# A folded last transform, a new end of attention, edge values by DMA, and two short products moved

## The chip, the cores and the metric

The kernel runs on one core of one Trainium2 chip. The metric is the device time of one execution in microseconds (us); all times here are in us unless marked otherwise.

## The reference, cut to what matters

Input `x` is (4, 16, 16, 192) in fp32: four images of 256 places and 192 channels. Four layers follow each other.

- Layer 0 and layer 2 are transformer blocks on windows of 14 x 14: norm, q, k, v, attention of 12 heads of 16 channels with relative positions in rows and columns, softmax, projection, residual; then norm, an MLP of 768 hidden channels with GELU, residual. 16 is not a multiple of 14, so each image gives one whole window and narrow windows on the right and at the bottom (the edges, filled up with padding).
- Layer 1 is a spectral layer with a 2-D real FFT over the places, a block-diagonal two-layer complex MLP, a soft threshold and the inverse FFT.
- Layer 3 is a spectral layer with a Hartley transform over all four axes (images, rows, columns and channels):

```python
def _dht(x):
    f = jnp.fft.fftn(x)
    return f.real + f.imag
X_k  = _dht(x);  X_nk = jnp.roll(jnp.flip(x, (1, 2)), (1, 1), (1, 2))
a, an = X_k[:, r0:r1, :kept], X_nk[:, r0:r1, :kept]          # 16 x 9 modes
o1_k  = relu(0.5*(a@w1[0] - an@w1[1] + a@w1[1] + an@w1[0]) + b1[0])   # o1_nk likewise
o2_k  = 0.5*(o1_k@w2[0] - o1_nk@w2[1] + o1_k@w2[1] + o1_nk@w2[0]) + b2[0]
o2_nk = 0.5*(o1_nk@w2[0] - o2_k@w2[1] + o1_nk@w2[1] + o2_k@w2[0]) + b2[1]
s = o2_k + o2_nk;  s = sign(s) * max(abs(s) - 0.01, 0)
out = _dht(full_with_s) / full.size + x
```

## The kernel before

Each engine has a written-out program of its own, and semaphores order them. The order of the work within an engine is the order in the code. All tensors stay on chip; the DMA queue of SyncE (SP) loads weights and stores the result.

**Attention (`attention(l)`, run for l = 0 and 1).** The tokens are 8 tiles of 128. The norm is done in two halves g of 4 tiles: VectorE takes means and variances (L1332, L1350, L1352), ScalarE the root (L1191), VectorE normalises (L1359), TensorE transposes (`turn_norm`, L751), and ScalarE and VectorE write the result with scale and bias to `yT` (L1196, L1338). `project` (L776) makes q and k: 3 chunks of 128 columns by 2 parts of 512 tokens. 192 channels are 128 and 64, so each of the 6 jobs has one whole product of 128 rows and one short product of 64 rows, both in L791; first all whole ones, then all short ones. `project_values` (L810, L816) makes v. Two jobs `v_edge` (L797) make v again for the edge places, out of a copy of `yT` in window order that POOL makes (L650). `relate` (L834) makes the relative terms, whose last take-out is VectorE's L1398. The list `PROJ` names these jobs; job j uses bank (4 + j) % 8 and waits until job j - 8 has been taken out.

Then 18 groups follow (`GROUPS`: slot of four heads by image or edge window). The edge groups are the 9th to the 14th. For each group TensorE makes scores (`score`, L875, banks 0 to 3), VectorE takes their maxima (L1408, L1411) and turns them (L1426), SP copies the turned maxima into rows of the operand by four DMAs (L628), TensorE makes the scores again transposed and with the maximum subtracted (`turn`, L903, banks 4 to 7), ScalarE takes exponentials (L1250), TensorE weighs the values (`weigh`, L916, bank 4, the last group bank 7), ScalarE takes that out (`take_weighed`, L1241), VectorE inverts the sums (`invert`, L1434 to L1440) and POOL divides (`divide`, L688 to L697). `out_project` (L762) follows per image. The last groups run without scores beside them. After the last `weigh` come `take_weighed`, ScalarE's table load for the root (L1187), the last `invert` and the second norm; then the MLP (L988, L1006), whose output VectorE adds to the residual (L1469).

SP's queue in an attention: four copies that move half of k between partitions (L615) after the take-out of chunk 2, a wait for POOL's first edge inputs (L616), then per group a wait and four copies of maxima (L628).

**Last transform (`spectral3`).** VectorE makes sums and differences of images (`mix`, L1520 to L1526). TensorE makes the flipped input (L1086), then for 4 mixes by 2 halves of channels a product over the places with 288 columns (real and imaginary, 144 modes each; L1096), VectorE's `unmix` (L1512 to L1515) and ScalarE (L1297) put them in `z`; L1106 is the transform over the channels with 4 products each; L1122 the first MLP, L1134 to L1147 the second (`o2k`, `o2nk`). VectorE adds, clips and subtracts (L1550 to L1556), mixes again (L1562 to L1567); L1153 and L1159 go back over the channels with 384 columns (cosines and sines of 192 channels), `unmix` follows, and L1171 goes back over the places. Four stores end the kernel.

The functions that the diff touches:

## Time and profile before

| | us |
|---|---|
| median of 3 runs (373.46 to 373.66) | 373.46 |
| the profiled execution | 375.45 |
| its span, first to last instruction | 373.3 |
| busy in the span: TensorE products / weight loads | 350.7 / 265.4 |
| busy in the span: VectorE / ScalarE / POOL | 198.9 / 147.7 / 99.5 |

The profiled execution has 2.15 outside the span of its instructions. All durations of single instructions come from it. A matrix product in fp32 is two instructions in the trace. A line of "chain of waits" is a piece of the work that ended last, followed back from the end. The profile says of an idle stretch what ended it; "issue" means that nothing in the profile did.

### The profile page before, as it was taken

What the parts mean: (1) busy time and instruction counts of PE and PEld (TensorE: products, weight loads), DVE (VectorE), ACT (ScalarE), POOL (GpSimd) and SP (SyncE); (2) the same over time, 40 slices, a digit from 0 to 9 for tenths busy, and PEclk for the clock granted to TensorE, in tenths of its full rate; (3) what the DMA queues carried; (4) which work ended last, traced back from release to release, by engine and by line L of the source; (5) the groups of instructions that cost most, each with busy time, mean ns of one, the idle gap of its engine ahead of it and who ended that gap; (6) DMA issues with size and microseconds to landing.
All of it is one profiled execution on the core that took longest, in us unless ns stands there. A gap on an engine that the chain in (4) does not pass through costs nothing.

```text
span 373.3 us, 10580 instructions
## 1 busy us (share of the span) xinstructions
PE 350.7 (94%) x4510; PEld 265.4 (71%) x4510; DVE 198.9 (53%) x476; ACT 147.7 (40%) x322; POOL 99.5 (27%) x189
## 2 busy tenths in 40 slices
PE   5899799999977999999899899999987999999996
PEld 3467688788855449979567688889865538987456
DVE  6363667777847401147851857777756600251562
ACT  2187055554544540140159045555554442021410
POOL 3100509983311066000000506985311030000000
PEclk9899999999999999999999999999999999999999
DMA  7970000000030012100201000000000000000002
GB/s 217 390 254 14 2 4 4 5 3 4 5 115 2 22 28 79 63 2 0 84 2 32 3 3 4 3 2 5 5 3 2 0 2 0 2 0 0 2 2 84
DMA packets 8958, 13.56 MB, mean 36 GB/s; under 512 B 3152, under 2 KB 6480, under 8 KB 8912
## 3 DMA queue, kind: packets, MB, share of 16 engines
q1 hardware_dynamic: 8912, 12.89, 10.5%
q8 instruction: 36, 0.59, 0.6%
q14 instruction: 10, 0.08, 0.1%
HBM read 11.46 MB, written 0.79 MB: 33 GB/s over the span
## 4 chain that ended last, share of the span: by engine, by line
PE 88%; DVE 7%; issue 1%; ACT 1%; SPq 1%; DMA 1%; DVEq 0%
PE banks L903 16%; PE banks L875 12%; PE banks L988 9%; PE banks L1006 8%; PE banks L916 8%; PE banks L834 6%; PE banks L791 4%; PE banks L762 2%; PE banks L751 2%; PE banks L1171 2%; PE banks L1096 2%; PE banks L1106 2%; PE banks L1019 2%; PE banks L1066 2%; DVE negmax L1408 2%; PE banks L810 2%
## 5 line engine op out<-in xcount | busy, mean ns | idle before, releaser
L1250 ACT ACTIVATE arena<-banks 128x392 f32<-128x392 f32 (+2 forms) x144 | 62.1, 486 | 62.4 <-PE banks L903 62.4
L875 PE MATMUL banks<-attention_arena 32*128 32x196 f32 x384 | 49.1, 353 | 3.1 <-DVE negmax L1408 1.6
L903 PE MATMUL banks<-attention_arena 32*128 32x196 f32 x384 | 47.5, 342 | 3.3 <-ACT arena L1250 2.0
L1411 DVE TENSOR_REDUCE negmax<-banks 128x4 f32<-128x784 f32 x40 | 39.0, 974 | 14.5 <-PE banks L875 14.3
L903 PE MATMUL banks<-attention_arena,keys 32*128 32x196 f32 x384 | 44.3, 323 | 0.0
L875 PE MATMUL banks<-keys,attention_arena 32*128 32x196 f32 x384 | 44.1, 323 | 0.0
L903 PEld LDWEIGHTS banks<-attention_arena 32*128 32x128 f32 x384 | 30.1, 183 | 10.3 <-issue 7.7
L988 PE MATMUL banks<-yT,fc 128*128 128x512 f32 (+1 forms) x96 | 33.3, 607 | 0.3
L916 PE MATMUL banks<-arena,v_and_ones 128*32 128x196 f32 (+2 forms) x672 | 30.9, 308 | 2.5 <-ACT arena L1250 2.4
L1006 PEld LDWEIGHTS banks<-fc,arena 128*128 128x128 f32 x192 | 31.1, 190 | 1.5 <-ACT arena L1265 1.5
L875 PEld LDWEIGHTS banks<-attention_arena 32*128 32x128 f32 x384 | 28.2, 183 | 5.6 <-DVE negmax L1408 3.3
L903 PEld LDWEIGHTS banks<-attention_arena,keys 32*128 32x128 f32 x384 | 32.1, 184 | 0.0
L1006 PE MATMUL banks<-fc,arena 128*128 128x192 f32 x192 | 31.7, 327 | 0.0
L875 PEld LDWEIGHTS banks<-keys,attention_arena 32*128 32x128 f32 x384 | 31.6, 184 | 0.0
L1469 DVE TENSOR_TENSOR x_tok<-banks,x_plus_bias 128x384 f32<-128x384 f32 x8 | 4.5, 558 | 48.4 <-PE banks L1006 48.4
L903 PE MATMUL banks<-edge_rel,edge_keys 32*128 32x112 f32 (+1 forms) x288 | 29.6, 278 | 0.0
L903 PE MATMUL banks<-edge_q,edge_k 32*128 32x112 f32 (+1 forms) x288 | 28.7, 274 | 0.0
L916 PEld LDWEIGHTS banks<-arena,v_and_ones 128*32 128x32 f32 x672 | 16.8, 109 | 12.8 <-ACT arena L1250 9.9
L988 PEld LDWEIGHTS banks<-yT,fc 128*128 128x128 f32 (+1 forms) x96 | 12.8, 188 | 18.3 <-issue 15.8
L690 POOL TENSOR_TENSOR divided_part<-o_and_sums,inverse_sums 128x196 f32<-128x196 f32 (+2 forms) x24 | 13.1, 546 | 46.2 <-DVE inverse_sums L1440 46.0
L903 PEld LDWEIGHTS banks<-edge_rel,edge_keys 32*128 32x128 f32 x288 | 22.6, 186 | 2.5 <-issue 2.5
L1416 DVE TENSOR_REDUCE negmax<-banks 112x2 f32<-112x560 f32 (+1 forms) x24 | 18.7, 780 | 9.3 <-PE banks L875 9.2
(164 smaller groups left out, 654.2 us busy)
## 6 DMA issues: line engine op xcount, KB each, us to landing
fc<-in_fc SPq DMA_DIRECT2D x2, 768.0 KB, 5.4
qkv<-in_qkv SPq DMA_DIRECT2D x2, 576.0 KB, 4.0
fc<-in_fc SPq DMA_DIRECT2D x2, 576.0 KB, 5.4
attention_arena<-negmaxT SPq DMA_DIRECT2D x72, 1.0 KB
rel<-in_rel SPq DMA_DIRECT2D x2, 448.0 KB, 4.6
x_tok<-in_x SPq DMA_DIRECT2D x4, 192.0 KB, 3.1
inverse<-in_inverse SPq DMA_DIRECT2D x1, 768.0 KB, 7.9
edge_rel<-negmaxT SPq DMA_DIRECT2D x48, 0.5 KB
```

The source lines that it names most:

```text
L690: pool.tensor_tensor(part, o, shape(m.inverse[:, ring]), ALU.mult).then_inc(s.divided, 1)
L751: last = nc.tensor.transpose(m.bank[bank0 + 2 * g + half][:, 128 * i:128 * (i + 1)], m.xn[:, 4 * g + i, REST * half:REST * half + 128], c[ ...
L791: ins = mm(bank[:, :], wl["qkv"][rows, half, 128 * g:128 * (g + 1)], m.yT[rows, half, 512 * part:512 * (part + 1)], start=not short, stop= ...
L834: ins = mm(bank[row(quad), 192 * n:192 * (n + 1)], wl["rel"][row(quad), 0 if kind == "rel_h" else 1, at % WIN], q[:, :, :, at], start=True ...
L875: ins = mm(o, asking, asked, start=not with_rel, stop=bool(with_rel))
L903: last = mm(m.bank[4 + j][:, cols * tile:cols * (tile + 1)], keys_of(slot, b, j, tile)[with_rel], queries_of(slot, b, j)[with_rel], start= ...
L916: last = mm(m.bank[weighed_in(n)][row(j), 0:cols], values_of(slot, b, j, tile), m.probsT[:, n % P_RING, j, cols * tile:cols * (tile + 1)], ...
L988: ins = mm(m.bank[j % 8][:, :], wl["fc1"][rows, half, 128 * hid:128 * (hid + 1)], m.yT[rows, half, 512 * g:512 * (g + 1)], start=not short ...
L1006: last = mm(m.bank[4 + b][:, CH * tile:CH * (tile + 1)], m.hidT[:, hid, at:at + 128], wl["fc2"][:, hid], start=hid == 0, stop=hid == HID_T ...
L1250: run(m.probsT[:, n % P_RING, j, 0:cols], m.bank[4 + j][:, 0:cols], ACT.Exp).then_inc(s.probs, 1)
L1411: dve.tensor_reduce(at[:, 4 * part:4 * part + 4].rearrange("k (j a) -> k j a", a=2), m.banks[:, 2 * part:2 * part + 2, 0:2 * MAIN_KEYS].re ...
L1416: dve.tensor_reduce(at[rows, 2 * part:2 * part + 2], m.banks[rows, 2 * part:2 * part + 2, 0:EDGE_KEYS[b - IMAGES]], AX, ALU.max, negate=Tr ...
```

## The change

**Projections.** The channels of x are put in another order on the host side of the layout (`PLACE`: 0 to 95, then 191 down to 96), and weights and biases with them. `project` runs: whole products of part 0, the second half's transposes, the short products of jobs 0 and 1, the whole products of part 1, the other four short products. The jobs `v_edge` and POOL's copies are gone; in their place SP copies rows of v between partitions, 5 DMAs per image, 20 per attention, and POOL sets two strips of v to zero at the start. PE waits for them at the first edge group.

**End of attention.** The weighing of the third last group goes to bank 2, that of the second last to bank 3, and they wait for their own exponentials and for all maxima instead of the next group's first exponential. `take_weighed` always stands between the two pairs of exponentials. The table load stands ahead of the last `take_weighed`, and the last `invert` inside the norm, behind the variance.

**Last transform.** Channel n and 192 - n are added and subtracted (`fold`, VectorE, after each image's MLP output), which gives 97 sums and 97 differences. The product over the places takes either with 144 columns and 97 rows of result; the one over the channels has 2 products instead of 4; the one back has 2 x 97 columns, and ScalarE and VectorE write the 192 channels from them in two pieces. The identity is added to `mix_diag`, so that `o2nk` comes out with `o2k` in it; the bounds of the clip have the bias in them, and the clip reads PSUM. The inverse of each image waits for its own inputs.

```diff
+PLACE = np.r_[0:HALF, CH - 1:HALF - 1:-1]
+FOLD = HALF + 1
 def weighed_in(n):
-    return 7 if n == N_GROUPS - 1 else 4
+    return {N_GROUPS - 3: 2, N_GROUPS - 2: 3, N_GROUPS - 1: 7}.get(n, 4)
...
+                wait_for(sp, s.proj_in, *taken_out(job("v", IMAGES - 1, 0)))
+                for b in range(IMAGES):
+                    for tile in range(2):
+                        rows = min(WIN - 8 * tile, 8)
+                        for col in range(EDGE):
+                            to, at = EDGE * (WIN * b + 8 * tile) + col, WIN + col
+                            sp.dma_start(m.v[to:to + EDGE * (rows - 1) + 1:EDGE, TILES], m.v[at:at + SIDE * (rows - 1) + 1:SIDE, 2 * b + tile])\
+                              .then_inc(s.v_moved, 16)
+                    low = EDGE * SIDE
+                    sp.dma_start(m.v[low * b:low * (b + 1), TILES + 1], m.v[128 - low:128, 2 * b + 1]).then_inc(s.v_moved, 16)
...
+            pool.tensor_tensor(f3.mix_diag[:], f3.mix_diag[:], c["ident"][:, :].unsqueeze(1).broadcast_to([128, 2, 128]), ALU.add).then_inc(weights_mixed, 1)
+            for n, side in enumerate((-LAMBDA, LAMBDA)):
+                pool.tensor_scalar(f3.bounds[:, n], f3.b[:, 6:8], -1.0, side, ALU.mult, ALU.add).then_inc(weights_mixed, 1)
...
-                for short in (False, True):
-                    for j in range(first, last):
+                for short, jobs in ((False, range(CHUNKS)), (True, range(2)), (False, range(CHUNKS, 2 * CHUNKS)), (True, range(2, 2 * CHUNKS))):
+                    if short and 0 in jobs:
+                        turn_norm(s.ln[0], 0, 1)
+                    for j in jobs:
...
                     if n >= 2:
-                        pe.wait_ge(s.pv_out, n - 1)
+                        pe.wait_ge(s.pv_out, min(n - 1, N_GROUPS - 3))
...
-                pe.wait_ge(s.probs, min(4 * (n + 1) + 1, 4 * N_GROUPS))
+                if weighed_in(n) == 4:
+                    pe.wait_ge(s.probs, 4 * (n + 1) + 1)
+                else:
+                    pe.wait_ge(s.probs, 4 * (n + 1))
+                    pe.wait_ge(s.max, 2 * N_GROUPS)
...
+                for n, mix in enumerate((3, 2, 0, 1)):
                     pe.wait_ge(S3.mixed, {3: 1, 2: 1, 0: 2, 1: 3}[mix])
+                    for part in range(2):
+                        for tile in range(2):
+                            last = mm(m.bank[n][0:FOLD, MODES * part:MODES * (part + 1)], m.mix[:, mix, tile, part],
+                                      c["space_cas"][:, tile, part ^ (mix == 3)], start=tile == 0, stop=tile == 1)
                     last.then_inc(S3.fwd.pe, 1)
...
-                    for n in range(4):
-                        last = mm(m.bank[4 + j][:, 0:2 * MODES], c["chan_fwd"][:, n // 2, n % 2, 128 * half:128 * (half + 1)],
-                                  m.z[:, n // 2, n % 2, 2 * g:2 * g + 2], start=n == 0, stop=n == 3)
+                    for part in range(2):
+                        last = mm(m.bank[4 + j][:, 0:2 * MODES], c["chan_fwd"][:, part, 128 * half:128 * (half + 1)],
+                                  m.z[0:FOLD, part, 2 * g:2 * g + 2], start=part == 0, stop=part == 1)
...
-                        if n > 0 and pair == (n + AHEAD >= N_GROUPS):
+                        if n > 0 and pair == 0:
                             take_weighed(n - 1)
+                load_table(ACT.Sqrt)
                 take_weighed(N_GROUPS - 1)
-
-                load_table(ACT.Sqrt)
...
-                invert(N_GROUPS - 1)
-                normalise(wl, s.ln[1], add_output, EPS[l], 4, 9, taken=2)
+                normalise(wl, s.ln[1], add_output, EPS[l], 4, 9, meanwhile=lambda: invert(N_GROUPS - 1), taken=2)
...
+            def fold(b):
+                if b == 0:
+                    dve.memset(m.folded[:, :, :, 1, 0::HALF], 0.0).then_inc(S3.folded, 1)
+                dve.wait_ge(A[1].fc2.dve, b + 1)
+                near, far = m.x[:, b, :, 1:HALF], m.x[:, b, :, HALF:CH - 1]
+                dve.tensor_tensor(m.folded[:, b, :, 0, 1:HALF], near, far, ALU.add).then_inc(S3.folded, 1)
+                dve.tensor_tensor(m.folded[:, b, :, 1, 1:HALF], near, far, ALU.subtract).then_inc(S3.folded, 1)
+                dve.tensor_copy(m.folded[:, b, :, 0, 0::HALF], m.x[:, b, :, 0::CH - 1]).then_inc(S3.folded, 1)
...
+                        total, clip = m.bank[2 * half + g][:, 0:2 * MODES], m.clip3[:, half, cols]
+                        dve.tensor_scalar(clip, total, f3.bounds[:, 0, half:half + 1], f3.bounds[:, 1, half:half + 1], ALU.max, ALU.min).then_inc(S3.clipped, 1)
                         dve.wait_ge(S3.clipped, 2 * half + g + 1)
+                        dve.tensor_tensor(m.s[:, half, cols], total, clip, ALU.subtract).then_inc(S3.shrunk, 1)
...
+                for b in (1, 3):
+                    re, im = m.gb[:, 0, b], m.gb[:, 1, b]
+                    dve.tensor_tensor(re[:, 0:HALF], g0[:, even], h1[:, even], ALU.add if b == 1 else ALU.subtract)
+                    dve.tensor_tensor(re[:, HALF:CH], g0[:, odd], h1[:, odd], ALU.subtract if b == 1 else ALU.add)
+                    dve.tensor_tensor(im[:, 0:HALF], g1[:, even], h0[:, even], ALU.subtract if b == 1 else ALU.add)
+                    dve.scalar_tensor_tensor(im[:, HALF:CH], g1[:, odd], -1.0, h0[:, odd], ALU.mult, ALU.subtract if b == 1 else ALU.add)\
+                       .then_inc(S3.back.dve, 1)
```

## Rows read from the trace of the kernel before

**Rows 1.** The profile's page: engine shares, and the granted clock in 40 slices.
```profile
PE 350.7 (94%) x4510; PEld 265.4 (71%) x4510; DVE 198.9 (53%) x476; ACT 147.7 (40%) x322; POOL 99.5 (27%) x189
...
PEclk9899999999999999999999999999999999999999
```
**Rows 2.** Chain of waits, second attention's projections: start, duration, work.
```profile
185.59 0.82 DVE yT L1338
...
186.55 5.59 PE banks L791 x18
...
196.44 1.36 PE banks L797 x8
```
**Rows 3.** Timeline, same stretch: start, duration, work [idle before, what ended it].
```profile
189.29 0.30 PEld L791 LDWEIGHTS banks<-yT,qkv 64*128 64x128 f32 x4 [0.76 <-issue]
...
195.51 0.74 DVE L1393 TENSOR_SCALAR attention_arena<-banks,vecs 128x512 f32<-128x512 f32 x1
```
**Rows 4.** Timeline of SP's queue, second attention, up to its first groups.
```profile
196.28 2.47 SPq L615 DMA_DIRECT2D attention_arena<-attention_arena  x4
212.36 9.24 SPq L628 DMA_DIRECT2D attention_arena<-negmaxT  x12
```
**Rows 5.** The issues of two source lines: ns least, median, most.
```profile
L615 SPq DMA_DIRECT2D attention_arena<-attention_arena x8: 576/590/732, 25.4 to 198.2; - x8
...
L628 SPq DMA_DIRECT2D edge_rel<-negmaxT x48: 497/497/572, 69.5 to 260.7; - x48
```
**Rows 6.** Chain of waits, end of the second attention.
```profile
285.55 0.93 PE banks L916 x16
...
286.50 0.34 ACT o_and_sums L1241
...
287.55 0.41 DVE inverse_sums L1440
...
288.26 0.42 DVE var_eps L1352
...
289.58 1.31 PE banks L751 x8
```
**Rows 7.** Timeline: POOL's last weight, and the end of the second attention.
```profile
145.74 0.85 POOL L738 TENSOR_SCALAR f_mix_nk<-f_mix_nk 128x256 f32<-128x256 f32 x1
...
278.66 0.88 PE L916 MATMUL banks<-arena,v_and_ones 128*32 128x196 f32 x16 [0.61 <-ACT arena L1250]
...
286.86 1.28 ACT L1187 ACT_TABLE_LOAD   x1
...
288.04 0.60 POOL L688 TENSOR_TENSOR attention_arena<-o_and_sums,inverse_sums 128x196 f32<-128x196 f32 x1 [1.69 <-DVE inverse_sums L1440]
288.15 0.20 ACT L1187 ACTIVATE spare<-spare 128x1 f32<-128x1 f32 x1
```
**Rows 8.** Chain of waits: first spectral transform, then the last transform's groups.
```profile
154.61 7.76 PE banks L1019 x32
...
329.17 7.81 PE banks L1096 x32
336.98 7.76 PE banks L1106 x32
...
356.01 2.58 PE banks L1153 x8
...
362.32 8.01 PE banks L1171 x48
```
**Rows 9.** Timeline of VectorE in the last transform.
```profile
326.42 0.90 DVE L1522 TENSOR_TENSOR arena<-x_tok 128x768 f32<-128x768 f32 x1
...
355.35 0.51 DVE L1550 SCALAR_TENSOR_TENSOR attention_arena<-banks,f_b,attention_arena 128x288 f32<-128x288 f32 x1
355.89 0.31 DVE L1554 TENSOR_SCALAR attention_arena<-attention_arena 128x288 f32<-128x288 f32 x1
...
359.43 0.17 DVE L1567 TENSOR_TENSOR attention_arena<-attention_arena 128x16 f32<-128x16 f32 x1
```

More of the change, by code:

```diff
@@ L791, in project @@
                             ins = mm(bank[:, :], wl["qkv"][rows, half, 128 * g:128 * (g + 1)], m.yT[rows, half, 512 * part:512 * (part + 1)],
-                                     start=not short, stop=short)
-                        elif kind == "v_edge":
-                            if not short and g == 0:
-                                pe.wait_ge(s.edge_inputs, Y_EDGES)
-                            n, half = EDGE_QUERIES[g], (j + short) % 2
-                            ins = mm(bank[0:n, 0:CH], m.yEdge[rows, half, g, 0:n], wl["qkv"][rows, half, 2 * CH:3 * CH],
                                      start=not short, stop=short)
@@ L1152, in spectral3 @@
                         pe.wait_ge(S3.hs, 6 * half + (1, 1, 3, 4)[n])
-                        last = mm(m.bank[4 + n][:, 0:2 * CH], m.hs[:, half, FULL * mix:FULL * (mix + 1)], c["chan_back"][:, half],
+                        last = mm(m.bank[4 + n][:, 0:2 * FOLD], m.hs[:, half, FULL * mix:FULL * (mix + 1)], c["chan_back"][:, half],
                                   start=half == 0, stop=half == 1)
@@ L1158, in spectral3 @@
                     for part in range(2):
-                        last = mm(m.bank[0][64 * part:64 * (part + 1), 0:CH], m.hs[:, half, LEFT_AT:],
-                                  c["chan_back"][:, half, CH * part:CH * (part + 1)], start=half == 0, stop=half == 1)
+                        last = mm(m.bank[0][64 * part:64 * (part + 1), 0:FOLD], m.hs[:, half, LEFT_AT:],
+                                  c["chan_back"][:, half, FOLD * part:FOLD * (part + 1)], start=half == 0, stop=half == 1)
                     if half:
@@ L1225, in attention @@
                             ins = run(v_values(2 * g + tile), bank[:, CH * tile:CH * (tile + 1)].rearrange("k (s h c) -> k s h c", s=SLOTS, c=HD), ACT.Copy)
-                    else:
-                        if l == 0:
-                            act.wait_ge(v_ones_set, 1 + SLOTS)
-                        n = EDGE_QUERIES[g]
-                        ins = run(v_values(TILES + g, slice(0, n)), bank[0:n, 0:CH].rearrange("k (s h c) -> k s h c", s=SLOTS, c=HD), ACT.Copy)
                     ins.then_inc(s.proj_in.act, 1)
@@ L1311, in spectral3, with unfold @@
                         bias=f3.b[:, 4 + half:5 + half]).then_inc(S3.o2k.act, 1)
[L1312 to L1318 removed]
+                even, odd = slice(0, HALF), slice(1, FOLD)
+                def unfold(mix):
+                    act.wait_ge(S3.back.pe, 3 + mix)
+                    for part in range(2):
+                        dst, src = m.gb[:, part, 2 * mix], m.bank[6 + mix][:, FOLD * part:FOLD * (part + 1)]
+                        run(dst[:, 0:HALF], src[:, even], ACT.Copy)
+                        ins = run(dst[:, HALF:CH], src[:, odd], ACT.Copy, scale=-1.0 if part else 1.0)
+                    ins.then_inc(S3.back.act, 1)
+                act.wait_ge(S3.back.pe, 1)
+                run(m.hpart[:, 0, 0:2 * FOLD], m.bank[4][:, 0:2 * FOLD], ACT.Copy).then_inc(S3.back.act, 1)
+                unfold(0)
+                act.wait_ge(S3.back.pe, 5)
+                run(m.gb_left[:, 0:HALF], m.bank[0][:, even], ACT.Copy)
+                run(m.gb_left[:, HALF:CH], m.bank[0][:, odd], ACT.Identity, scale=f3.b[:, 8:9], bias=f3.b[:, 9:10]).then_inc(S3.back.act, 1)
+                unfold(1)
             act.wait_ge(spare_set, 1)
@@ L1470, in attention @@
                        .then_inc(s.fc2.dve, 1)
+                    if l == 1:
+                        fold(b)
             def spectral1():
@@ L1592, in _split, with _placed @@
     return np.stack([v[:128], v[REST:]], 1)
+def _placed(blocks):
+    out = blocks[[0, 1, 2, 3, 7, 6, 5, 4]]
+    out[4:] = out[4:, ::-1]
+    if out.ndim > 2:
+        out[4:] = out[4:, :, ::-1]
+    return out
 def _pair(blocks, half, r, at=0):
@@ L1685 @@
     result = run_bass_kernel_spmd(nc, [arrays], core_ids=[0])
-    return result.results[0]["out"]
+    return result.results[0]["out"][..., np.argsort(PLACE)]
```

203 lines of the change are left out of this document (91 added, 112 removed).

## The prediction

> **What bounds the kernel now.** Read the engine shares first, then the granted clock: TensorE has work for 94% of the span and the clock stands at its upper level (2.4 GHz) in nearly every slice [rows 1]. The chain of waits, in order of time, is a row of TensorE groups with short links of other engines between them. So an edit is worth what it takes out of TensorE's row or out of a link, as long as nothing else becomes later than TensorE. Three stretches are touched: the projections of both attentions [rows 2, 3], the last groups of both [rows 6, 7], and the last transform [rows 8, 9]. Both attentions show the same pattern; I work on the second and count it twice.
>
> **Projections.** *Two short products.* The transposes end at 185.55, the norm's second half (0.82) is written, and the products of L791 run from 186.55 for 5.59 [rows 2]: 18 instructions, of which 6 are whole (128 rows) and 12 short (64 rows, two side by side). That is 12 places, 0.43 each as worked out below. Jobs 0 and 1 need only the first half of the norm. Their short products, 4 instructions in 2 places, 0.86, can run in the 1.0 gap. But the array now goes from whole to short to whole once more. At such a change the weight loads stand idle for 0.76 [rows 3]; the products lose less: an instruction of 288 columns takes 0.244 (7.81 / 32 [rows 8]), so one of 512 takes 0.43 and 12 places 5.2 of the 5.59, which leaves some 0.2 for a change of mode or a start. So the pair ends at about 185.55 + 0.22 + 0.86 = 186.63 and the whole products start at 186.85, 0.3 late; then 0.86 is gone behind them. Net -0.55 (bounds -0.86 and -0.2).
>
> The Trainium skill, page "TensorEngine Tiling (Array Packing)", section Key Properties, says that changing the tiling mode drains TensorE, which speaks against this edit; the trace agrees with it only as far as that 0.2 to 0.5, and by a rule without a price the edit would be taken as anything down to nothing.
>
> *Edge values.* The eight instructions of L797 leave the chain: 1.36 [rows 2]. One of its two changes of mode stays, 0.15. So -1.2 (bounds -1.0 and -1.36). The four POOL copies that fed them end far ahead of TensorE's use and cost nothing either way.
>
> *Does TensorE's next work wait?* `relate` waits for VectorE's last take-out of chunk 2, which starts at 195.51 and takes 0.74 [rows 3]. Job 1 is now taken out alone in the gap (one instruction, 0.72 of VectorE's row) and the products come 0.5 earlier, so it ends near 195.6; TensorE arrives near 195.9 + 0.15. It is in time by some 0.4. ScalarE takes the values out right behind.
>
> *What replaces them: 20 DMAs per attention on SP.* They stand in SP's queue behind the four k copies and ahead of the copies of the row maxima, and group 0's scores cannot be turned before those have landed. Today SP begins the k copies at 196.28 and the first maximum at 212.36, 16.1 later [rows 4]. In the new kernel the k copies begin 0.65 earlier and the maximum is ready 1.75 earlier, which leaves 15.0. The k copies take 2.5 of it [rows 4]; 12.5 stay for 20 issues, 0.62 each. The trace has no copy of this shape. The nearest: 0.50 for a copy from a few strided partitions, 0.59 for 16 partitions at 4 KB, with a longest of 0.73 [rows 5], plus 0.05 between issues. I take 0.55 for the sixteen copies of 6 or 8 partitions and 0.64 for the four of 32: 11.4. They fit with 1.1 to spare, cost 0. Bounds: all at 0.55, 0; all at 0.78, 15.6, which is 3.1 late per attention. What is late passes through: TensorE's turn of group 0 already follows the landing closely. The values themselves are wanted only at the ninth group, tens of us later.
>
> Sum: -1.75 per attention, -3.5 for both.
>
> **End of attention.** Today each of the last two turns is followed by a wait of 0.61 for the first exponential, since the next weighing writes bank 4 (before 278.66 [rows 7]; the other stands 4.5 later). Banks 2 and 3 take it away, so the weighing starts at once. ScalarE now takes the weighed values out between its two pairs of exponentials; the first pair (0.9) ends about when the weighing does (0.9), so the last exponential ends near 280.2, while `out_project(0)` keeps TensorE until 280.5. No new wait; the two turns end 0.45 and 0.93 earlier, and the last weighing starts near 284.55 instead of 285.55 [rows 6].
>
> Behind it, today: take-out 0.34, inversion to 287.96, then means, variance (0.42), root, reciprocal, first normalised tile, transposes at 289.58 [rows 6], 3.1 after the last weighing's end. New: it ends at 285.45; ScalarE has begun its table load (1.28) [rows 7] and the small activation (0.20) at 284.35 and is free only at 285.85, so the take-out comes 0.35 late and ends at 286.2; the inversion to 287.3, while means, variance and root are already made; reciprocal 0.22, tile 0.39: transposes at about 287.95, 1.6 earlier. Against this: `divide` on POOL (0.60) now falls on the reciprocal and the tiles. VectorE's variance of 4 elements took 0.42 today and ended 0.04 behind POOL's 0.60 [rows 6, 7]. If the same holds the first tile up, it costs 0.5. I take 0.2 of it: -1.4 per attention, -2.8 in all (bounds -1.0 and -1.6 each).
>
> The Trainium skill, page "SBUF — State Buffer", section Who interferes with whom, says that VectorE in a two-port mode and POOL lock each other out for a whole instruction. The row of the variance agrees; by that rule alone the tiles would be held only if they ran in such a mode, and the sum would be -1.6 or -1.1.
>
> **Last transform.** All of it is TensorE's row at full clock [rows 1, 8]. *Forward:* 16 products of 288 columns (32 instructions, 7.81) become 16 of 144, since the half with index 97 and up is not computed: at 0.244 per 288 columns an instruction takes 0.122, 3.9 for all, -3.9. *Channels:* 16 products of 288 become 8: 7.76 to 3.88, -3.9. *Between:* unchanged, 344.74 to 356.01, because the identity added to the diagonal weights costs no product.
>
> *Cover of the folding.* Three small VectorE instructions per image, of 190 and 4 elements, about 0.7. For images 0 to 2 they lie under the second MLP product. For image 3 they push the first mixed sum (0.90, starting at 326.42) to about 327.0 [rows 9]; it ends at 327.95 and TensorE wants it at 329.17 [rows 8], 1.2 later. The second pair of sums is ready 329.4 to 330.0, wanted at 331.1. Without that cover the price would be 0.7. *POOL* gets three more weights to prepare behind 145.74 + 0.85 [rows 7], about 1.4; they are wanted past the first spectral transform, which runs from 154.61 for 7.76 [rows 8]: hidden by 14.
>
> *Backward.* TensorE: 8 products of 384 columns become 194, and the left modes 192 become 97: 356.01 to 362.32 is 6.3 today [rows 8]; each product falls from 0.65 to 0.33. But the last ones wait for VectorE. Per group of modes it made a sum out of PSUM (0.51), a clip (0.31) [rows 9] and a difference; now a clip out of PSUM, taken as the 0.51 of the sum, and the difference. Second half: it could start at 355.35 [rows 9]; now near 355.05, the second group at 356.1 when TensorE gives it, and the last fold of the half ends at 358.8 instead of 359.6 [rows 9]. TensorE's last product then ends near 359.35. VectorE's eight half-width pieces of the unmixing (0.2 apart; each between 0.17 for 16 elements and 0.51 for 288 [rows 9]) start at 358.85; the first four release image 1 at 359.7. ScalarE has the left modes by 360.0, before TensorE's third product of that image. So the inverse starts at 359.75 instead of 362.32 [rows 8]: -2.55 (bounds -1.8, if each small piece costs 0.1 more on both engines, and -2.9). The inverse (8.0), the last sum and the store stay.
>
> Sum: -3.9 - 3.9 - 2.55 = -10.35.
>
> **Total.** 3.5 + 2.8 + 10.35 = 16.65. The profiled execution took 375.45 with a span of 373.3; it should come out near 358.8 with a span near 356.7. The median of the runs shown, 373.46, is 2.0 below it; the same difference gives 356.8.
>
> **Rivals.** *A. SP's queue becomes late* (chance 0.14): issues at 0.64 to 0.78. For: 0.59 and 0.73 are in the rows, and the new copies are strided on both sides. Against: the strided rows show 0.50. Loss 0.3 to 3.1 per attention: 357.4 to 363, middle 359.8. *B. The tail is cut less* (0.15): the small pieces of VectorE and ScalarE, with waits between, become the row that sets the end, and the end of attention is held up by POOL. For: VectorE is the last link into the inverse. Against: TensorE itself fills the two transforms. Price 0.75 + 2 x 0.4 and some 0.5 at the folding: near 358.8. *C. More than forecast* (0.09): all terms at their far bounds, 0.3 + 0.3 + 0.4 + 0.35: 355.4. *D. Slower than before* (0.03): the 20 copies cost far more to issue than any in the trace. It decides from (12.5 + 8.3) / 20 = 1.04 each, since two attentions must lose 16.65; at 1.2 each it would be 380. No row is above 0.73. *E. No measurable change* (0.01): the chain is not as read, and the products removed were hidden; only if SP's copies cost just that 1.04.
>
> My forecast has 0.58, with its own range 355.6 to 358.2.
>
> **Range.** Down to 355.0 for C, up to 360.0, which takes in B and most of A; above it stays the worse half of A and D, about 0.1, and below it about 0.05. 0.2% is 0.75, about what a measurement of this kernel can tell from no change. Faster 0.95, same 0.01, slower 0.04.
>
> **What would show it.** No L797 group; `relate` starting some 1.75 earlier after the transposes; SP's twenty issues at 0.55, ended before the first maximum of group 0; the two 0.6 waits ahead of the weighings gone, and transposes 2.5 after the last weighing's end instead of 3.1; the forward group at 3.9 and the channel group at 3.9; the inverse starting 3.8 after the o2 products. Wrong it would be if the maxima's copies start late behind the values', if an instruction of 144 columns takes well over 0.122, or if VectorE's row from the o2 products to the inverse has not become shorter.

## The result and the profile after

The changed kernel took 364.02 us (median of 4 executions, 362.36 to 364.9) against 373.56 for the kernel before in the same set: ratio 0.973, 95% interval 0.968 to 0.978. In a second set of six executions beside the experiments it took 362.03 (360.62 to 364.77) against 373.65: 0.968, 0.963 to 0.973. It is faster, by 9.5 to 11.6 us, where 16.65 were forecast, and the time is outside the forecast range of 355.0 to 360.0.

The profiled execution of after took 364.86 with a span of 362.9, 10.4 less than before. First the page of after: the shares of the chain that ended last.

```profile
PE 78%; SPq 10%; DVE 6%; issue 2%; ACT 2%; DMA 2%
```

Before, this chain had 88% PE and 1% SPq. A tenth of this chain now runs over SyncE's queue (SPq). Timeline of that queue in the first attention of after (start, duration, line, work, count):

```profile
24.93 3.65 SPq L620 DMA_DIRECT2D attention_arena<-attention_arena  x4
28.70 2.77 SPq L629 DMA_DIRECT2D v_and_ones<-v_and_ones  x4
...
41.92 0.56 SPq L632 DMA_DIRECT2D v_and_ones<-v_and_ones  x1
42.59 17.24 SPq L645 DMA_DIRECT2D attention_arena<-negmaxT  x20
```

The 20 copies of values fill 28.70 to 42.59, 13.9 us or 0.69 each; in the second attention they fill 198.45 to 213.11, 14.7. The row maxima (L645) go out behind them. Answers on the issues of two lines, ns least/median/most:

```profile
L629 SPq DMA_DIRECT2D v_and_ones<-v_and_ones x32: 568/671/1747, 28.7 to 211.7; - x32
...
L632 SPq DMA_DIRECT2D v_and_ones<-v_and_ones x8: 564/565/929, 31.5 to 212.4; - x8
```

The copies of 6 or 8 strided partitions cost more (0.67) than those of 32 neighbouring ones (0.565). Next the chain of waits in the first attention:

```profile
42.59 0.61 SPq L645
...
44.41 1.53 DMA attention_arena<-negmaxT
...
46.07 0.43 PE banks L915 x2
```

And TensorE's timeline at the first turn of each attention, with the idle time before it and what ended it, and below the first weighing behind each:

```profile
46.07 0.43 PE L915 MATMUL banks<-attention_arena 32*128 32x196 f32 x2 [3.00 <-DMA attention_arena<-negmaxT]
...
52.65 0.87 PE L934 MATMUL banks<-arena,v_and_ones 128*32 128x196 f32 x16
...
216.59 0.43 PE L915 MATMUL banks<-attention_arena 32*128 32x196 f32 x2 [2.53 <-DMA attention_arena<-negmaxT]
...
223.12 0.87 PE L934 MATMUL banks<-arena,v_and_ones 128*32 128x196 f32 x16
```

TensorE stands still for 3.00 and 2.53 us, where before it waited 0.65. From the first product of `relate` to this turn it is now 21.02 and 20.54 (starts at 25.05 and 196.05) against 18.70 in both attentions before (26.81 to 45.51, 197.73 to 216.43): 2.32 and 1.84 late. From the turn to the first weighing it is 6.58 and 6.53, before 4.98 in both. The windows of after show why that stretch grew (window, length, busy time and count of PE, PEld, DVE, ACT, POOL, granted clock, DMA share, GB/s):

```profile
44.00:46.00 2.00, 0.00 (x0) 0.00 (x0) 0.34 (x1) 0.00 (x0) 0.00 (x0) 1.00 0.01 1
46.00:48.00 2.00, 1.93 (x36) 1.96 (x40) 0.00 (x0) 0.00 (x0) 0.00 (x0) 0.81 0.01 2
48.00:50.00 2.00, 2.00 (x29) 2.00 (x29) 1.19 (x2) 0.89 (x2) 0.00 (x0) 0.50 0.03 8
50.00:52.00 2.00, 2.00 (x44) 2.00 (x43) 0.97 (x1) 0.89 (x2) 0.00 (x0) 0.84 0.01 2
52.00:54.00 2.00, 2.00 (x47) 1.38 (x44) 1.19 (x2) 1.21 (x3) 0.00 (x0) 1.00 0.00 0
```

Behind the stop the granted clock is at 0.50, the level of 1.2 GHz, for some 3.4 us, and it is so again from 217.9 to 221.3. Before, it was at 1.00 in all these windows. So the new queue costs 2.32 + 1.84 of waiting and 1.60 + 1.55 of slow products, 7.3 us in all.

The rest of the change did what it was to do. *Projections:* from the first transposes to `relate` 184.73 to 196.05, 11.32, against 184.24 to 197.73, 13.49 (rows next to [rows 2]): 2.17 less, forecast 1.75. The row of L791's products in the chain of after:

```profile
186.04 5.75 PE banks L809 x18
```

*End of the second attention*: first the line of before's chain from which it is measured, then the chain of after, to be held against [rows 6, 7]:

```profile
273.76 0.81 PE banks L916 x16
```

```profile
275.36 0.81 PE banks L934 x16
...
287.49 0.17 DVE var_eps L1370
...
288.75 0.70 DVE normed L1377
...
289.50 1.31 PE banks L769 x8
```

From the fourth-last weighing to the transposes it is 14.14 (275.36 to 289.50), before 15.82 (273.76 to 289.58): 1.68 less, forecast 1.4. Of that, 1.35 comes ahead of the last weighing, where the two waits of 0.61 are gone (it starts 10.43 behind the fourth-last one, before 11.78), and 0.32 behind it. The variance takes 0.17 and not 0.42, but the first normalised tile takes 0.70, before 0.39: POOL's last division runs at 288.73 for 0.60. *Last transform*, chain of waits of after, against [rows 8]:

```profile
329.08 3.94 PE banks L1111 x32
333.02 3.88 PE banks L1121 x16
...
348.18 1.31 PE banks L1168 x8
349.50 0.32 PE banks L1174 x4
349.81 1.71 PE banks L1168 x8
351.52 0.32 PE banks L1174 x4
351.84 8.10 PE banks L1189 x48
```

Forward 3.94 and channels 3.88 where 3.9 each was forecast; the inverse starts 3.66 behind the o2 products, forecast 3.75, before 6.31. From the first product of the transform to the end of the span 325.56 to 362.9, 37.34, before 325.64 to 373.3, 47.66: 10.3 less, forecast 10.35.

The sum of the trace: 10.3 + 2 x 2.17 + 2 x 1.68 = 18.0 gained, 7.3 lost on the queue and the clock, 0.4 later at the start (first q, k products at 9.66, not 9.25). That is 10.3; the spans differ by 10.4.

### The profile page after: what moved, and what is told of

It is laid out like the page before. It is cut to its first block, busy times and chain, and to the rows that moved or that the text cites. A ratio compares the mean times of both kernels' runs of the same rounds, so it can differ in the third digit from the quotient of the medians.

```text
span 362.9 us, 10569 instructions
## 1 busy us (share of the span) xinstructions
PE 340.8 (94%) x4478; PEld 264.4 (73%) x4478; DVE 199.7 (55%) x483; ACT 146.1 (40%) x322; POOL 99.1 (27%) x186
## 4 chain that ended last, share of the span: by engine, by line
PE 78%; SPq 10%; DVE 6%; issue 2%; ACT 2%; DMA 2%
PE banks L915 17%; PE banks L887 12%; PE banks L1005 9%; PE banks L1023 9%; PE banks L934 8%; SPq L629 6%; PE banks L809 4%; PE banks L780 2%; PE banks L769 2%; PE banks L1189 2%; PE banks L1036 2%; PE banks L1083 2%; SPq L632 1%; PE banks L1053 1%; PE banks L1137 1%
## 5 line engine op out<-in xcount | busy, mean ns | idle before, releaser
L915 PE MATMUL banks<-attention_arena 32*128 32x196 f32 x384 | 49.4, 353 | 7.6 <-DMA attention_arena<-negmaxT 5.5
L887 PE MATMUL banks<-attention_arena 32*128 32x196 f32 x384 | 50.9, 362 | 3.1 <-DVE negmax L1426 1.6
L915 PE MATMUL banks<-attention_arena,keys 32*128 32x196 f32 x384 | 46.2, 334 | 0.0
L887 PE MATMUL banks<-keys,attention_arena 32*128 32x196 f32 x384 | 46.2, 334 | 0.0
L915 PEld LDWEIGHTS banks<-attention_arena 32*128 32x128 f32 x384 | 32.0, 192 | 14.5 <-issue 11.5
L887 PEld LDWEIGHTS banks<-attention_arena 32*128 32x128 f32 x384 | 30.3, 192 | 5.5 <-DVE negmax L1426 3.3
L915 PEld LDWEIGHTS banks<-attention_arena,keys 32*128 32x128 f32 x384 | 33.6, 191 | 0.0
L887 PEld LDWEIGHTS banks<-keys,attention_arena 32*128 32x128 f32 x384 | 33.2, 191 | 0.0
L667 POOL COPY edge_rel<-attention_arena 128x112 f32<-128x112 f32 x6 | 1.4, 278 | 91.3 <-DVE attention_arena L1416 91.3
```

Source lines behind the costliest of these rows:

```text
L887: ins = mm(o, asking, asked, start=not with_rel, stop=bool(with_rel))
L915: last = mm(m.bank[4 + j][:, cols * tile:cols * (tile + 1)], keys_of(slot, b, j, tile)[with_rel], queries_of(slot, b, j)[with_rel], start= ...
```

## The experiments

**Theory.** SyncE's 20 copies ahead of the first maxima stop TensorE, and the stop takes the clock down. **Rivals.** The copies slow the attention by their traffic, wherever they stand; the clock fall has a cause of its own; part of the loss sits in the other parts of the change. Differences below are to the kernel before, timed beside each kernel.

**Three copies behind each group (a1_spread).** In this cut and the next the count is written into the call.

```
-                # all 20 value copies ahead of group 0's maxima
+                move(0)
                 for n, (slot, b) in enumerate(GROUPS):
                     ...  # the four copies of the maxima
+                    move(3)
```

> The changed kernel with SyncE's 20 copies of values issued three at a time behind each group's row maxima (groups 0 to 6, the last two copies behind group 6) instead of all 20 ahead of group 0's. Nothing else differs. Theory 1 (SyncE's queue is late for group 0, TensorE stands still for 3.0 and about 2.5 us at the first turn of each attention, and the granted clock falls behind that stop): both losses go, 2 x (2.1 + 1.6) = 7.4 us, so 356 to 357.5; TensorE has no idle above 1 us ahead of its first turn and the clock stays at 1.00 in all windows behind it; the later groups lose nothing, since their pitch of 3.79 us leaves SyncE room for three more issues of 0.6 to 0.7 beside four of 0.5. Theory 2 (the copies themselves slow the attention, by their traffic beside TensorE's work, wherever they stand in the queue): the loss is only moved into groups 1 to 7, 361 to 364, with a longer pitch there. Theory 3 (only the wait is SyncE's, the clock fall has another cause, such as the start of the group pipeline): 4.2 us back, about 360, and the clock still falls to 0.50 behind the first turn.

Measured: 367.2 us, ratio 0.978 (0.973 to 0.983), 7.6 us below before: no better than the changed kernel, and against all three expectations as I had priced them. Timeline of SyncE's queue in this kernel:

```profile
43.81 2.31 SPq L652 DMA_DIRECT2D attention_arena<-negmaxT  x4
46.17 1.96 SPq L637 DMA_DIRECT2D v_and_ones<-v_and_ones  x3
48.17 2.28 SPq L652 DMA_DIRECT2D attention_arena<-negmaxT  x4
50.49 2.10 SPq L637 DMA_DIRECT2D v_and_ones<-v_and_ones  x3
```

The stop at the first turn is gone (0.65 again), but a group now costs SyncE 4.36 to 4.46 us, and TensorE's group takes 3.79. Seven groups at 0.57 to 0.67 too much are 4.0 to 4.7 per attention, more than the 3.7 per attention that the missing stop and the clock behind it save. My expectation had written down both numbers of that sum and not added them. This profile also has a slow stretch of the clock in another place (table below). The run can't tell the queue from traffic; the next two can.

**One copy behind each group, 13 ahead (c1_split).** The same with `move(13)` and `move(1)`.

> The changed kernel with 13 of SyncE's 20 copies ahead of group 0's row maxima and then one behind each group's maxima (groups 0 to 6). The run with three copies behind each group had no stop at the first turn, but SyncE's row became the bound of the attention: 2.3 us of maxima plus 2.0 of copies is 4.4 us per group against TensorE's 3.79. One copy per group makes 2.3 + 0.7 = 3.0, below 3.79, and 13 copies at 0.69 end 9 us behind the k copies, before the first maxima are ready at 14.5 behind their start. Theory 1 (what matters is only where SyncE's row stands against TensorE's): no wait of TensorE for the maxima above 0.2, the group pitch 3.79, and the whole 7.3 us is back: 0.978 less 0.4 points of the changed kernel on this chip, that is about 7 us below it, 356 to 358. Rival (the copies cost by their traffic): no more than half of it back, 360 or above.

Measured: 356.18 (355.17 to 358.57), ratio 0.952 (0.948 to 0.956): 17.5 below before and 5.9 below the changed kernel of the same set. All 20 copies are still made, and their traffic with them. SyncE's queue in this kernel:

```profile
28.20 8.75 SPq L637 DMA_DIRECT2D v_and_ones<-v_and_ones  x13
37.65 2.33 SPq L652 DMA_DIRECT2D attention_arena<-negmaxT  x4
40.02 0.71 SPq L637 DMA_DIRECT2D v_and_ones<-v_and_ones  x1
...
43.08 0.56 SPq L637 DMA_DIRECT2D v_and_ones<-v_and_ones  x1
44.62 2.22 SPq L652 DMA_DIRECT2D attention_arena<-negmaxT  x4
```

Here SyncE is ahead: it waits for the maxima (36.95 to 37.65, 43.64 to 44.62). `relate` to first turn is 18.67 (22.98 to 41.65), as before the change, and no window ahead of the end has a clock below 1.00. This is the version that beats both kernels.

**The copies on another queue (c2_gpsimd_queue).**

```
-                sp.dma_start(m.v[to:...], m.v[at:...]).then_inc(s.v_moved, 16)      # and its 19 likes
+                pool.dma_start(m.v[to:...], m.v[at:...]).then_inc(s.v_moved, 16)    # behind edge(0), edge(1)
```

> The changed kernel with the 20 copies issued by GpSimd instead of SyncE, behind the preparation of the first two edge groups, where GpSimd's row is empty from 41.5 to 58.2 us in the profile of the changed kernel. Theory 1: SyncE has only the k copies and the maxima, so no stop at the first turn, 356 to 358, if GpSimd issues one in less than 16.7 / 20 = 0.83 us; slower issues push its first division and with it the weighed values, and the price then shows as waits on GpSimd's products from group 2 on: at 1.2 us each 7 us late, of which its slack behind the first groups takes some, 358 to 364. Rival (the copies cost by their traffic): 360 or above with the wait gone.

Measured: 356.35 (355.08 to 358.25), ratio 0.952 (0.947 to 0.957), the same as c1_split. GpSimd's issues in this kernel, ns:

```profile
L711 POOL DMA_DIRECT2D v_and_ones<-v_and_ones x32: 529/550/777, 41.8 to 218.5; - x32
```

The block ends at 52.8, ahead of the first division (54.69). So the copies by themselves cost nothing here: the rival of their traffic falls.

**TensorE kept busy in the wait (a2_filler).** Four products whose result is used by nothing.

```
+                for _ in range(4):
+                    mm(m.bank[4][:, 0:2 * MAIN_KEYS], m.q[:, 0, 0:128], m.q[:, 0, 0:2 * MAIN_KEYS], start=True, stop=True)
                 pe.wait_ge(v_ones_set, 1 + SLOTS)     # then the first turn
```

> The changed kernel with four extra products (eight instructions of 392 columns, about 2.7 us, their result is used by nothing) put ahead of the first turn of each attention, where TensorE otherwise stands still. Nothing else differs, so the wait for the row maxima ends when it did. Theory 1: with TensorE kept busy the granted clock does not fall, 1.00 in the windows behind the turn; the first turn begins at the same time, the first weighing follows it after 5.05 us instead of 6.6; 2 x 1.6 = 3.2 us less, near 361. Rival (the slow stretch behind the turn is not the clock's answer to the stop, but waits or DMA traffic that would be there anyway): 364, the stretch from first turn to first weighing still 6.6.

Measured: 361.88 (360.02 to 362.44), ratio 0.965 (0.960 to 0.970), 12.9 below before. The stops shrink to 0.76 and 0.50; the turns are as late as ever (21.4 behind `relate` in the first attention), and the first weighing follows them after 4.99 in both. The profile has the clock at 1.00 behind both turns, and a fall in another place, at the second-last turn of the second attention. TensorE's timeline and windows there:

```profile
274.00 0.91 PE L915 MATMUL banks<-attention_arena 32*128 32x196 f32 x8 [1.01 <-ACT arena L1265]
```

```profile
272.00:274.00 2.00, 0.99 (x12) 0.63 (x8) 1.86 (x7) 1.22 (x3) 0.46 (x1) 1.00 0.02 5
274.00:276.00 2.00, 2.00 (x26) 2.00 (x30) 0.02 (x1) 0.00 (x0) 0.60 (x1) 0.55 0.01 1
276.00:278.00 2.00, 2.00 (x29) 0.98 (x23) 0.00 (x0) 0.89 (x2) 0.00 (x0) 0.60 0.03 8
```

That stop of 1.0 stands in both attentions of every kernel here, before included. In the 13 profiles, 26 such stops, the clock fell behind four (in a1_spread, a2_filler, b1_only_short and b2_only_end) and held behind 22. So the wait and the clock are two prices, as the theory has it, but the second is paid only some of the time. That is also why this run by itself doesn't show that the filler kept the clock up: of the six long stops at a first turn without filler (after, c3_after_again, a4_only_copies), three held too. What ties the fall to the stop is the count over all profiles: in the nine that wait only 0.65 to 0.68 there, the clock stands at 1.00 from the turn to the first weighing in all 18 attentions.

**Edge values projected again (a3_edges_projected).** One part of the change undone.

```
-PROJ += [("v", n, 0, "act") for n in range(IMAGES)]
+PROJ += [("v", n, 0, "act") for n in range(IMAGES)] + [("v_edge", n, 0, "act") for n in range(2)]
-                    for col in range(EDGE):
-                        sp.dma_start(m.v[to:...], m.v[at:...]).then_inc(s.v_moved, 16)
+                        pool.tensor_copy(as_window(m.yEdge[:, half, e], e), window(m.yT[:, half], e)).then_inc(s.edge_inputs, 1)
+                        ins = mm(bank[0:n, 0:CH], m.yEdge[rows, half, g, 0:n], wl["qkv"][rows, half, 2 * CH:3 * CH], ...)
```

> The changed kernel with one part undone: the edge groups' values are projected again by TensorE (eight instructions per attention, out of copies that GpSimd makes), and SyncE copies no values. The two other parts and the folded transform stay. Theory 1: 1.36 us per attention comes back to TensorE's row, the loss of 3.65 per attention goes: 364 - 7.3 + 2.7, about 359.5; no idle above 1 us ahead of the first turn, the clock at 1.00 behind it. Theory 2 (the loss belongs to the other parts, such as the short products in the norm's gap or the new end of attention): 364 or above.

Measured: 359.97 (358.33 to 361.19), ratio 0.960 (0.955 to 0.965), 14.8 below before, where 14.0 was expected. No wait for the maxima is left. The loss belongs to the copies on this queue. The kernel that never had them is 4.5 to 5.8 us ahead of the changed one between the two points of the table below; the interval of its ratio lies below that of the changed kernel's first set and overlaps a little with that of the second.

**The copies alone (a4_only_copies).** The kernel before with that part and nothing else: its diff is in essence that of a3_edges_projected read the other way, on the kernel before.

> The kernel before with one part of the change alone: the edge groups' values are copied by 20 DMAs on SyncE's queue instead of being projected. Theory 1: 1.2 to 1.4 us per attention saved in the projections, but the row maxima of group 0 go out late, and the clock falls behind the stop. Here TensorE arrives about 0.9 us later than in the changed kernel relative to the norm, since the two short products are not ahead, while SyncE's row starts as before: a wait of 1.5 to 3 us and 1 to 1.6 us for the clock per attention, so 374 to 378, slower than the kernel before. Rival (copies fit and cost nothing, the changed kernel loses elsewhere): 371, faster by 2.6.

Measured: 376.5 (374.11 to 377.12), ratio 1.003 (1.000 to 1.007), 1.7 above before, an interval that just holds no change. In the profile the first turns are 1.93 and 0.69 late, 2.6 in all, against two times 1.36 saved: the part gives back what it saves, and that it is slower than before isn't shown. TensorE's timeline and windows in this kernel:

```profile
48.17 0.43 PE L906 MATMUL banks<-attention_arena 32*128 32x196 f32 x2 [2.62 <-DMA attention_arena<-negmaxT]
```

```profile
48.00:50.00 2.00, 1.82 (x44) 1.86 (x48) 0.10 (x1) 0.18 (x1) 0.00 (x0) 1.00 0.01 2
50.00:52.00 2.00, 2.00 (x54) 2.00 (x50) 1.82 (x3) 1.51 (x4) 0.00 (x0) 1.00 0.03 8
```

A stop of 2.62, longer than one after which the changed kernel's clock fell, and the clock holds. The second attention's stop is 1.37, and it holds there too.

**The copies alone, issued by GpSimd (d1_only_copies_gpsimd).** The same with the edit of c2_gpsimd_queue on top.

> The kernel before with the copies of values alone, as in the run with that part alone, but issued by GpSimd behind the preparation of the first two edge groups, at 0.55 us each as the last runs showed. If the idea of the part is sound and only its queue was wrong, TensorE keeps the 1.36 us of the edge products per attention and waits for nothing: 1.2 to 1.4 less per attention, 2.4 to 2.8 in all, 0.993 of before. If moving values by DMA costs beside the queue, 0.998 or above.

Measured: 372.27 (370.51 to 374.42), ratio 0.993 (0.990 to 0.996), 3.0 below before. The same part that gains nothing on SyncE's queue (1.7 above before) saves 3.0 on GpSimd's.

**The changed kernel once more (c3_after_again).** No edit.

> The changed kernel once more, unaltered, as the reference on the chip of these runs and for a second profile of it. Theory 1: the stops at the two first turns are there again, 3.0 and about 2.5 us, since they follow from SyncE's count of copies. Of the granted clock: if its fall is the answer to the stop, it is at 0.50 behind both stops again; if it falls at times of its own, it stands elsewhere or nowhere in this profile, and the time varies with the run's mean clock, by about 1.7 us for each 0.0045 of it. The kernel with copies alone had stops of 2.6 us with the clock at 1.00 behind them, so I give the second 0.6. Time 362 to 366.

Measured: 362.03, the second set told above, with a second profile. (The copies alone had one stop of 2.6, not two, as the text above has it.) Its stops are 3.69 and 1.37; windows of the first:

```profile
40.00:42.00 2.00, 0.66 (x4) 0.36 (x3) 1.24 (x2) 0.00 (x0) 0.00 (x0) 1.00 0.15 38
42.00:44.00 2.00, 0.00 (x0) 0.00 (x0) 0.00 (x0) 0.00 (x0) 0.00 (x0) 0.54 0.01 2
44.00:46.00 2.00, 1.65 (x20) 1.68 (x24) 0.00 (x0) 0.00 (x0) 0.00 (x0) 0.50 0.01 2
46.00:48.00 2.00, 2.00 (x31) 2.00 (x28) 0.54 (x1) 0.62 (x2) 0.00 (x0) 0.50 0.03 8
```

The clock fell inside the first stop and stayed down twice as long; behind the second it held. The six executions of this set, time with the run's mean granted clock: 360.62 and 360.67 at 0.995, 361.2 at 0.990, 362.87 at 0.991, 364.58 and 364.77 at 0.981. One stretch of 3.4 us at half clock is 1.7 / 361 = 0.005 of the mean, so these are about 1, 2 and 4 such stretches, wherever they stand (a stretch at the start of the kernel counts too), and three more cost 4.1 us. None of the ten executions of the changed kernel had a mean of 1.000; two of four of a3_edges_projected and four of six of c1_split were at 0.999 or 1.000.

**The other parts alone.** Short products (b1_only_short), new end of attention (b2_only_end), folded last transform (b3_only_folded), each added alone to the kernel before.

```
# b1_only_short
-                for short in (False, True):
-                    for j in range(first, last):
+                order = ((False, range(CHUNKS)), (True, range(2)), (False, range(CHUNKS, 2 * CHUNKS)), (True, range(2, 2 * CHUNKS)))
...
+                for short, jobs in order:
...
+                    for j in jobs:
# b2_only_end, with the change's order of take-outs, of the table load and of the inversion
-    return 7 if n == N_GROUPS - 1 else 4
+    return {N_GROUPS - 3: 2, N_GROUPS - 2: 3, N_GROUPS - 1: 7}.get(n, 4)
# b3_only_folded, with the change's folded forward, channel and unmixing steps
-                        last = mm(m.bank[4 + n][:, 0:2 * CH], m.hs[:, half, FULL * mix:FULL * (mix + 1)], c["chan_back"][:, half],
+                        last = mm(m.bank[4 + n][:, 0:2 * FOLD], m.hs[:, half, FULL * mix:FULL * (mix + 1)], c["chan_back"][:, half],
```

> The kernel before with the two short q, k products in the norm's gap alone. The prediction has 0.55 per attention. The trace of the changed kernel gave 2.17 for short pair and edge products together, where 1.75 was forecast; if the edge products are worth 1.36, the pair is worth 0.8: 1.6 less than before, 0.996. If the rest was the edge products', 0.55 per attention: 0.997.

> The kernel before with the new end of attention alone. The prediction has 1.4 per attention, the trace of the changed kernel 1.74: 2.8 to 3.5 less than before, 0.9915 on the middle. If the end's gain needs the copies or the short pair (it uses nothing of theirs), less than 2: 0.995 or above.

> The kernel before with the folded last transform alone; both attentions are as before. By the prediction's term, and by the trace of the changed kernel, 10.35 us less than before on the same chip: 363 to 364.5. Rival (the folded transform costs less because the new end of attention hands over earlier or later, so that alone it gives another sum): 9 or less, or over 11.

Measured: b1 374.82, ratio 0.998 (0.995 to 1.001), 0.4 below before, an interval that holds both expectations and no change as well; b2 372.31, 0.993 (0.989 to 0.997), 2.9 below; b3 364.95, 0.975 (0.970 to 0.980), 8.7 below, by itself the number of b3's rival (9 or less), though the interval reaches to 11.3. Times alone don't settle terms this small, since the executions of one kernel spread by up to 5.5 us. The profiles say more. From `relate` of the first attention to the end of the span, which leaves the start and the first projections out:

| kernel | `relate` to end, us | against before | slow stretches in it |
|---|---|---|---|
| before | 373.3 - 26.81 = 346.5 | | 0 |
| after | 362.9 - 25.05 = 337.9 | -8.6 | 2 |
| c3_after_again | 359.2 - 22.64 = 336.6 | -9.9 | 1, long |
| a1_spread | 365.9 - 24.68 = 341.2 | -5.3 | 1 |
| a2_filler | 360.5 - 23.13 = 337.4 | -9.1 | 1 |
| a3_edges_projected | 359.0 - 26.92 = 332.1 | -14.4 | 0 |
| c1_split | 353.5 - 22.98 = 330.5 | -16.0 | 0 |
| c2_gpsimd_queue | 356.1 - 25.43 = 330.7 | -15.8 | 0 |
| a4_only_copies | 375.3 - 27.54 = 347.8 | +1.3 | 0 |
| d1_only_copies_gpsimd | 368.9 - 23.73 = 345.2 | -1.3 | 0 |
| b1_only_short | 372.9 - 25.97 = 346.9 | +0.4 | 1 |
| b2_only_end | 373.4 - 28.61 = 344.8 | -1.7 | 1 |
| b3_only_folded | 362.6 - 26.32 = 336.3 | -10.2 | 0 |

With 1.7 off for a slow stretch, b2 is at -3.4 (two ends of 1.7), b1 at -1.3 (one short pair), d1 at -1.3 (one set of edge products). The second end of b2, timed like that of after, is 1.66 shorter than before's. The chains give the projections of the second attention directly, first transposes to `relate`: b1 184.68 to 197.40, 12.72, 0.84 less than before's 13.56 by the chain; d1 181.17 to 193.37, 12.20, 1.36 less. Together 2.20, and the changed kernel shows 2.17. So the parts add up (two ends, one set of projections, since the first lies ahead of `relate`): -10.2 - 3.4 - 2.2 = -15.8, and the two kernels with the queue mended show -15.8 and -16.0.

## Why the prediction was wrong

*The step that failed* is the cost of SyncE's 20 copies: "I take 0.55 for the sixteen copies of 6 or 8 partitions and 0.64 for the four of 32: 11.4. They fit with 1.1 to spare, cost 0." They took 0.67 and 0.565 and, with what lies between two issues, 13.9 and 14.7 for the 20, against the room of 12.5. In the first attention the k copies also took 3.65, not the 2.65 of the same stretch before. The lateness was 2.32 and 1.84, inside my own bound of 3.1. I had chosen the value by the likeness of strided partitions, and the strided row with 0.50 is a copy of another shape; the wide row [rows 5] was nearer in cost. With 1.1 to spare out of 12.5, and 0.59 and 0.73 in the rows, the step was no better than even, and I gave rival A 0.14. It was rival A, in the upper half of its range. These 4.2 us alone would have made 356.8 into 361.0, past the range.

*The term that was missing* is the clock. What I called "passes through" was priced at the length of the wait. A wait of 2 to 3 us can also take the clock to half for some 3.4 us, 1.6 per attention here. With it the sum is 364.1; the 1.3 that the other terms gave beyond their forecast and the 0.4 at the start leave 363.2, against the 364.02 measured in the first set and 362.03 in the second. Rows for it were there: the kernel before has such a stretch in its second slice of the clock [rows 1], behind a stop of 1.86 us at the start (TensorE's timeline of before):

```profile
9.25 4.51 PE L791 MATMUL banks<-yT,qkv 128*128 128x512 f32 x6 [1.86 <-DVE yT L1338]
```

The Trainium skill, page "TensorE: Matmul & The Clock Gate", section Part 1: The HAM clock gate, says that the clock follows TensorE's recent activity, seen in intervals that run on without regard to the program. By that rule one and the same stop may or may not cost the clock, depending on where it falls. The profiles agree: it fell in or behind stops of 3.69, 3.00 and 2.53 us and held behind one of 2.62 and two of 1.37, and it fell behind 4 of the 26 stops of 1.0 us ahead of an attention's second-last turn.

*Projections:* the mechanism was right, both terms a little small: 0.84 for the short pair (forecast 0.55) and 1.36 for the edge products (forecast 1.2). The changes of mode that I charged, 0.2 and 0.15, do not show: in the chain of after the transposes, the 18 products (5.75) and the values follow one another without a gap. The rule of a drain at a change of tiling mode, which the prediction took from the Trainium skill, page "TensorEngine Tiling (Array Packing)", section Key Properties, has at most 0.16 here for the added changes, the 5.75 against the 5.59 of [rows 2].

*End of attention:* 1.68 for 1.4, a little over my bound of 1.6. The mechanism was right; the part ahead of the last weighing was worth 1.35 where I had 1.0, the part behind it 0.32 where I had 0.4. The first tile beside POOL's division took 0.3 longer (0.70 against 0.39), where I had taken 0.2 out of a possible 0.5.

*Last transform:* right in all three terms: 3.87, 3.88 and 2.65 less for 3.9, 3.9 and 2.55, together 10.3 for 10.35, with the trace of b3_only_folded at 10.2. VectorE's clip out of PSUM took 0.58 where I had 0.51, and was not late for it.

*The total* without the failed step: c1_split 356.18 and c2_gpsimd_queue 356.35, where 356.8 was forecast; that is 17.5 and 17.3 below before, for 16.65.

## What to carry to other kernels

Add up a DMA queue like an engine: issues times the cost of one against the time between its first and its last due date, and again per turn of the steady loop; if the spare is less than the spread of the issue costs in the trace, expect it to be late. Put small copies that are due late behind or between those that are due early, or on an engine whose row is empty. Where an edit makes TensorE stop for one to three microseconds, price a stretch at half clock with it, as a chance (here 3 of 6 stops of 1.4 to 3.7 us, 4 of 26 of 1.0), and compare profiles between two points inside the program, not whole times.

## What the runs showed of the hardware

- An issue of a copy within the core's memory costs the issuing engine some 0.5 us or more: on SyncE 0.50 for a row of maxima [rows 5], 0.67 for 6 or 8 strided partitions, 0.565 for 32 neighbouring ones; on GpSimd 0.55 and 0.54 for the same two. The Trainium skill, page "DMA: Bandwidth & Descriptors", section Issuing engines are not separate DMA queues, says that starting DMAs from several engines only saves the time of the issue, usually small beside the transfer itself. Here the issue is what bound: 20 of them made 13.9 us. The same page's section Issuing engine by pattern calls the path of SyncE's DMAs generally the faster, without saying in what; the time on the issuing engine was the other way round here, 0.67 against 0.55.
- A kernel without the long stops also spreads by 3 to 4 us (a3_edges_projected, c1_split, c2_gpsimd_queue, d1_only_copies_gpsimd). The start is a good part: `relate` began between 22.64 and 28.61 us, and the first six q, k products are a part of that: 2.84 us in four profiles, 4.5 to 5.5 in the seven where the windows show the clock at 0.50 there. TensorE's timelines of c1_split and a3_edges_projected:

```profile
9.25 2.84 PE L817 MATMUL banks<-yT,qkv 128*128 128x512 f32 x6 [1.19 <-DMA qkv<-in_qkv]
```

```profile
9.61 5.10 PE L800 MATMUL banks<-yT,qkv 128*128 128x512 f32 x6 [1.24 <-DVE yT L1367]
```

- In a3_edges_projected and c2_gpsimd_queue these six took 5.10 though every window there shows the clock at 1.00. A single one took 1.06 us (median), as in the half-clock windows of before, and 0.59 in c1_split; the DMA traffic is alike (348 to 423 GB/s). So I read them as a slow stretch that the granted clock doesn't record. A mean clock of 1.000 then doesn't rule out a slow start, one more reason to compare from `relate` on. Why it is missing from the record stays open.
- What decides whether the clock falls behind a given stop was not tried; its length alone does not (2.62 held, 2.53 and some of 1.0 did not).
